# Row maxima of attention scores as pairs of 64-row matmuls on the two row halves of TensorE's array

## What is computed

```python
q = q.reshape(B * NUM_HEADS, S, hd)          # 8 heads of 64 values, S = 1024 tokens
k = k.reshape(B * NUM_HEADS, S, hd)
v = v.reshape(B * NUM_HEADS, S, hd)
scores = jnp.einsum('gqd,gkd->gqk', q, k) / jnp.sqrt(jnp.asarray(hd, x.dtype))
attn = jax.nn.softmax(scores, axis=-1)
wv = jnp.einsum('gqk,gkd->gqd', attn, v)
```

## Time and profile before

| | |
|---|---|
| median of 3 runs | 2581.28 us (2579.69 to 2582.69) |
| profiled execution, its time | 2579.7 us |
| profiled execution, its span | 2577.9 us |
| mean granted TensorE clock | 0.997 of full speed |
| busy share of PE, DVE, ACT, POOL | 97%, 75%, 44%, 44% |
| the chain that ended last: PE, DVE, issue, DMA | 86%, 5%, 2%, 2% |

### The profile page before, as it was taken

How to read it: one execution, slowest core, us unless ns; L and a number is a source line. 1 busy time by engine, 2 the same in 40 slices (tenths; PEclk the granted TensorE clock), 3 DMA queues, 4 the chain that set the end, 5 groups by cost and what they waited for, 6 DMA issues and landing times.

```text
span 2577.9 us, 39692 instructions
## 1 busy us (share of the span) xinstructions
PE 2501.4 (97%) x11720; PEld 987.6 (38%) x11720; DVE 1939.5 (75%) x2647; ACT 1141.6 (44%) x2059; POOL 1128.4 (44%) x971
## 2 busy tenths in 40 slices
PE   6999999999999999999999999999999999999999
PEld 2333333333333333333333333333344444444444
DVE  5887787778788787777878798976866966967515
ACT  4455555555545545555555554556232132132100
POOL 1366566556546746655664664655112021030000
PEclk9999999999999999999999999999999999999999
DMA  5234153242433315333342533332434634633534
GB/s 159 72 84 119 62 130 85 68 123 62 116 97 100 98 47 139 86 92 104 78 119 64 133 96 84 104 89 86 174 144 145 248 131 169 239 131 131 196 108 170
DMA packets 209915, 301.71 MB, mean 117 GB/s; under 512 B 82208, under 2 KB 131488, under 8 KB 209696
## 3 DMA queue, kind: packets, MB, share of 16 engines
q1 hardware_dynamic: 209424, 297.97, 38.9%
q10 hardware_dynamic: 272, 1.05, 0.1%
HBM read 195.54 MB, written 52.69 MB: 96 GB/s over the span
## 4 chain that ended last, share of the span: by engine, by line
PE 86%; DVE 5%; issue 2%; DMA 2%; ACT 1%; SPq 1%; POOL 1%; DVEq 0%; ACTq 0%; POOLq 0%
PE bank L846 29%; PE bank L752 16%; PE bank L726 14%; PE bank L687 11%; PE bank L705 8%; PE bank L697 6%; DVE nmax L1280 2%; PE bank L715 1%; DMA q_b<-shift 1%; DVE prob_sum L1274 1%; ACT prob L929 1%; PE bank L739 1%; SPq L419 1%; DVE qk_lo L1266 1%; DMA den_col<-den_sb 0%
## 5 line engine op out<-in xcount | busy, mean ns | idle before, releaser
L1280 DVE TENSOR_REDUCE nmax<-bank 128x1 f32<-128x512 f32 x1024 | 657.9, 682 | 231.7 <-PE bank L705 227.4
L929 ACT ACTIVATE prob<-bank 128x512 f32<-128x512 f32 x1024 | 560.7, 593 | 496.9 <-PE bank L726 492.5
L846 PE MATMUL bank<-v,u_slab 128*128 128x512 f16 x3456 | 746.9, 379 | 0.0
L1109 POOL TENSOR_TENSOR prob_sum<-prob_sum,prob 128x512 f32<-128x512 f32 x354 | 502.7, 1420 | 370.2 <-ACT prob L929 369.2
L752 PE MATMUL bank<-prob,val 128*64 128x512 f32 x2048 | 496.6, 606 | 0.0
L846 PEld LDWEIGHTS bank<-v,u_slab 128*128 128x128 f16 x3456 | 338.1, 98 | 407.0 <-issue 0.8
L705 PE MATMUL bank<-k_a,q_a 128*128 128x512 f16 x1024 | 384.2, 383 | 14.5 <-DVE nmax L1280 6.8
L1274 DVE TENSOR_TENSOR prob_sum<-prob_sum,prob 128x512 f32<-128x512 f32 x354 | 357.7, 1011 | 3.5 <-issue 0.3
L726 PE MATMUL bank<-q_a,k_a 128*128 128x512 f16 x1024 | 315.5, 381 | 16.6 <-ACT prob L929 15.0
L726 PE MATMUL bank<-q_b,k_b 128*128 128x512 f16 x1024 | 305.6, 380 | 9.0 <-DMA q_b<-shift 8.9
L752 PEld LDWEIGHTS bank<-prob,val 128*64 128x64 f32 x2048 | 124.3, 136 | 248.5 <-issue 206.4
(11 more groups left out here) (142 smaller groups left out, 2588.1 us busy)
## 6 DMA issues: line engine op xcount, KB each, us to landing
u_slab<-u_scratch SPq DMA_DIRECT2D x72, 1024.0 KB, 5.0
xs<-x SPq DMA_DIRECT2D x28, 1024.0 KB, 5.6
tile<-x_scratch SPq DMA_DIRECT2D x26, 1024.0 KB, 6.9
u_scratch<-u_w SPq DMA_DIRECT2D x96, 192.0 KB, 2.8
q_a<-qk_hi SPq DMA_DIRECT2D x64, 256.0 KB, 4.8
den_sb<-recip_scratch SPq DMA_DIRECT2D x128, 128.0 KB, 2.9
x_scratch<-xr SPq DMA_DIRECT2D x16, 1024.0 KB, 4.6
xr<-x SPq DMA_DIRECT2D x15, 1024.0 KB, 7.6
```

Source lines behind the costliest of these rows:

```text
L846: mm = pe.matmul(bank_at(pos, co)[:].rearrange("p (i n) -> p i n", i=2), slab[:, l, c, co * P:(co + 1) * P], image[v][:, 2 * c:2 * c + 2, ...
L929: act.activation(prob[:, (2 * u + e) % 8], sc_bank[bank_turn(s * 16 + 2 * u + e, 16 * HPI)[0]][:], ACT.Exp, scale=float(D) ** -0.5).then_i ...
L1109: nc.gpsimd.tensor_tensor(acc, in0, prob[:, (2 * kc + 1) % 8], ALU.add).then_inc(s1["sum1"], 1)
L1280: dve.tensor_reduce(nmax[:, m // 2, m % 2:m % 2 + 1], src[:], AX.X, ALU.max, negate=True)\
```

## The change

Each maximum tile now uses q's high part and k's high part only, 64 rows of products for a tile, and two tiles are issued one after the other: one on rows 0 to 63 (`k_b` against `q_a`), one on rows 64 to 127 (`k_a` against `q_a`), into two banks of the ring. For this the two parts of k change places in `k_a`; both halves of `q_a` hold the same, so the scores stay as they are. Places a and b are gone; `MAX_AT` puts a pair either at c (behind the unit's scores, ahead of d and of the burst) or at the new place e, behind the burst. DVE reduces two tiles for each pair.

```diff
-MAX_QUOTA = [2, 3, 3, 3, 3, 2, 0, 0]
+MAX_AT = {(0, "c"): 0, (0, "e"): 1, (1, "c"): 2, (2, "c"): 3, (2, "e"): 4, (3, "c"): 5, (4, "c"): 6, (4, "e"): 7}
...
-                hi_to = ((k_a, 0), (k_b, 0)) if which == 0 else ((q_a, 0), (q_a, D))
-                lo_to = (k_a, D) if which == 0 else (q_b, 0)
+                hi_to = ((k_a, D), (k_b, 0)) if which == 0 else ((q_a, 0), (q_a, D))
+                lo_to = (k_a, 0) if which == 0 else (q_b, 0)
...
-            def max_tile(s, m):
+            def max_pair(s, n):
 
                 half, tok = tokens(s)
-                dst = take()
-                pe.matmul(dst[:].rearrange("p (k t) -> p k t", t=TOK), q_a[half][:, m // 2, tok],
-                          k_a[half][:, 4 * (m % 2):4 * (m % 2) + 4, tok],
-                          start=True, stop=True).then_inc(s1["ring_full"], 1)
+                dst = take(), take()
+                for e, k_op in enumerate((k_b, k_a)):
+                    rows = slice(e * D, (e + 1) * D)
+                    pe.matmul(dst[e][:].rearrange("p (k t) -> p k t", t=TOK), q_a[half][rows, n, tok],
+                              k_op[half][rows, 4 * e:4 * e + 4, tok],
+                              start=True, stop=True).then_inc(s1["ring_full"], 1)
...
-                    run("a")
                     scores(h, s, u, 0)
-                    run("b")
                     if u == 0:
                         pe.wait_ge(s1["shift_row"], 16 * (h + 1))
                     scores(h, s, u, 1)
...
+                    run("e")
...
-                    for place in "abcd":
+                    if u == 1 and den_direct(s - 1, more):
+                        den_from_bank(h - 1)
+                    for place in "cde":
...
-                                max_item(h + 1, a)
+                                max_item(h + 1, 2 * a)
+                                max_item(h + 1, 2 * a + 1)
```

More of the change, by code:

```diff
@@ L102, in ring_items @@
 def ring_items(u, nxt, prev, v_units, stat):
-    first = sum(MAX_QUOTA[:u])
-    tiles = [("max", first + k) for k in range(MAX_QUOTA[u])] if nxt else []
-    at = {"a": tiles[0:1], "b": tiles[1:2], "c": tiles[2:]}
+    at = {place: [("max", MAX_AT[u, place])] if nxt and (u, place) in MAX_AT else [] for place in "ce"}
     at["d"] = [("value", u // 2)] if v_units and u % 2 else []
@@ L774, in run @@
                             if kind == "max":
-                                max_tile((s + 1) % HPI, a)
+                                max_pair((s + 1) % HPI, a)
                             elif kind == "value":
@@ L814, in _ @@
             pe.wait_ge(s1["qk_moved"], 192)
-            for m in range(16):
-                max_tile(0, m)
-                if m % 4 == 1:
-                    project_qk(1, 1, 0, m // 4)
+            for n in range(SEG):
+                max_pair(0, n)
+                if n % 2 == 0:
+                    project_qk(1, 1, 0, n // 2)
             slot(0, 0, prev=False)
@@ L1569, in slot @@
                             add_tile(h, s, u - 1)
-                        if place == "a" and u == 1 and den_direct(s - 1, more):
-                            den_from_bank(h - 1)
                         if place == "d" and u in (1, 2) and (s == 0 and ahead or s == 1 and more):
```

## The result

The changed kernel takes 2681.04 us (median of 4 runs, 2673.84 to 2685.36) where the kernel before takes 2581.04 beside it: ratio 1.0384, 95% interval 1.0360 to 1.0408. It is slower by 100 us; the prediction said 2600, in a range of 2554 to 2635. The sign was right, the size was a fifth of what came.

What follows compares the result with a forecast made beforehand. The prediction took PE as setting the pace, with DVE close in some slots. Slot terms summed to +2.5 us an image; six images +15 and the last two +5, on 2579.7, gave 2600, range 2554 to 2635.

Steps and rivals of the forecast that it cites:

- The price of a pair: On PE: two row-half matmuls run together in 0.23 us, and each change of the array's division costs 0.10.
- the gain of the quiet slots: Slots 4, 5, 2 and 6: the late reciprocal is covered, so they gain 0.6, 0.6, 0.5 and 0.5 us.
- The halves overlap: On PE: assumed in the sum; the rival without overlap said slower, 2665 us at most, chance 0.10.
- the one of free changes: Rival on PE: row halves change for less than 0.10 us, faster, 2560 or 2518, chance 0.12.
- Pair 5's wait for the ring: Slots 0 and 1: DVE reaches pair 4 late, so pair 5 waits for a bank, +0.75 us each.
- what the new order makes late: Main term: DVE's later reciprocal delays SP's queue and the shift; PE waits 3.5, 0.7, 1.3, 0.8 us in slots 1, 0, 3, 7.
- The lateness is harmless: Rival: the shift still lands in time in slots 0, 1, 3 and 7; faster, 2558 us, chance 0.20.
- the price of the lateness: Net change forecast per slot: +2.4 us in slot 1, +0.8 in 0, +1.0 in 3, +0.5 in 7.
- level with it: Slot 1, DVE: the reciprocal, 2.8 us ahead of the last burst before, would end together with that burst.
- the denominators' item: Slots 3 and 7, on PE: this item waits 0.16 us for a ring bank, part of why PE gains only 0.3.
- in any case: Slot 0: PE loses 0.80 us at the branch of the loop over images, whatever the change does.
- +5 for two: Last two images, where DVE also has the convolution's first tiles: 0 to +8 us, taken as 5.

Runs made afterwards that it cites:

- e3: The kernel before with only its reciprocal moved late, behind unit 5's last maxima: 2661.22 us, ratio 1.0335.
- e1: The changed kernel with the reciprocal moved early again, ahead of the reductions of unit 4's last pair: 2602.55 us, ratio 1.0082.
- e12: The changed kernel with only slot 0's 1 MB load issued behind the shift's send: 2663.43 us, ratio 1.0322.
- e5: The changed kernel with extra, later overwritten score products issued ahead of slots 2, 0 and 4 to fill the shift waits: 2674.36 us, ratio 1.0366.
- e10: e4 with the last image's maxima as full products in the places of the kernel before, and its reciprocal at the end of unit 4: 2583.18 us, ratio 1.0014.
- e6: The changed kernel, reciprocal still late, with the 1 MB loads of slots 0 and 1 issued behind the shift's send: 2625.76 us, ratio 1.0182.
- e4: e1 with the 1 MB loads of slots 0 and 1 issued behind the shift's send: 2596.05 us, ratio 1.0065.
- e11: e10 with pairs only in slots 2, 4, 5 and 6, the other slots having the maxima of the kernel before: 2563.82 us, ratio 0.9939.
- e9: The kernel before with only the 1 MB loads of slots 0 and 1 issued behind the shift's send: 2579.44 us, ratio 0.9994.

## Why the prediction came out wrong

**Right.** The price of a pair (0.22) and of a change (0.10); the gain of the quiet slots, -0.6 forecast and -0.7 measured in 4 and 5, -0.4 in 6. The halves overlap, so that rival is gone, and the one of free changes too. Pair 5's wait for the ring in slots 0 and 1, 0.75 forecast: it is 0.69 idle in both slots in every image from the second to the sixth. The row in slot 0 has 0.69, or 0.76 start to start (1008.43 - 1007.14 - 0.53):

```profile
1007.14 0.59 PE L726 MATMUL bank<-q_b,k_b 128*128 128x512 f16 x2
1008.43 0.39 PE L705 MATMUL bank<-k_b,q_a 64*128 64x512 f16 x1 [0.69 <-DVE nmax L1279]
```

The main term, "what the new order makes late", named the right mechanism, and in slots 1, 3 and 7 the right wait: e3 shows that lateness alone makes +82, e1 that taking it away returns the loop to 218.8. In slot 0 another wait counts: the reciprocal ends 1.8 ahead of the last burst (1.3 was written), and in the five passages with a gap at the branch PE does not wait for the shift at all, where 0.7 was forecast; it waits 1.3 only at the sixth, which has no gap. So slot 0's +2.8 is in the main the longer gap (2.6 to 3.0 idle for 0.8 to 1.6) and pair 5's wait. "The lateness is harmless" (0.20) was wrong.

**The step that failed: the price of the lateness**, forecast at 2.4, 0.8, 1.0 and 0.5 in slots 1, 0, 3 and 7, measured as 5.9, 2.8, 2.9 and 2.5. Six things were missing from it or sized too small.

- *The reciprocal came later than walked.* Against the last burst it ends 0.6 after in slot 1 (1053.98 - 1053.40; "level with it" was written) and 0.4 after in slots 3 and 7 (0.1 was written). So the shift waits, by the starts, are 4.3 to 4.7 in slot 1 (3.5), 1.5 to 2.2 in slot 3 (1.3) and 1.8 to 2.2 in slot 7 (0.8). Part of it is in the walk through DVE's queue: a split of 1.58 stands ahead of the reciprocal in slot 1, where the kernel before has 0.68 in the same place. (The prediction's own terms for slot 1, a landing at 10.0 and a need at 6.3, make 3.7 and not 3.5.)
- *The shift lands later.* The prediction gave it 2.2 in slots 3 and 7. It takes 2.1 to 2.8 from slot 3 and 2.9 to 3.2 from slot 7 in the loop. In slot 7 this is the larger part of the miss: 0.7 to 1.0, where the late reciprocal has 0.3.
- *The ring in slot 3.* The prediction had 0.16 for the denominators' item. That wait is there (0.19), but pairs 1 and 2 wait too: 0.7 to 1.1 in all.
- *The loop's branch.* The prediction had 0.80 there "in any case". It is not a constant: it changes with how long ahead the load was issued, and a late reciprocal moves the load to the worst of the four places seen. e12, which moves that load alone, takes 18 us off.
- *The clock.* Behind each of slot 1's shift waits (4.2 us and more) and each of the five gaps at the branch TensorE's granted clock is 0.5, which is 1.2 GHz, for a while. Behind the shorter waits (1.0 to 2.1 idle) it is so in three of seven images in slot 7 and in two of seven in slot 3. It costs 1.7 us in slot 2 alone (e5), and up to 5.2 in the image shown (PE's busy time). Over the whole execution the granted clock is 0.981 against 0.997, so the low clock has 43 of the 100 us at most. That is how slot 2, forecast at -0.5, came to +1.3. The Trainium skill ("TensorE: Matmul & The Clock Gate", "HAM oscillation — how this bites in real kernels") describes such a case, a wait for a DMA that lets the clock fall, so that the stage behind it starts at half rate every time; the trace agrees behind slot 1, with a burst of 3.68 for 1.94. It belonged in the sum as soon as a wait of 3.5 was forecast.
- *The last images.* +5 for two was taken by feel; it was +25 (19.6 and 5.3). e10 shows that 11 (by the table) to 13 (by the runs) of it are the places of the maxima in the last image. The 5.3 of the last but one are the lateness, since e1 has only 0.5 there.

What the 100 us are, by the runs in this order (in the other order, e1 ahead of e4, the reciprocal has 78 and the loads 6.5): 55 are the loads behind which a late reciprocal puts the shift and the branch's fetch (e6); 30 more the late reciprocal by itself (e6 to e4, 2625.8 to 2596.1); 13 the last image (e4 to e10); and 3 remain, since the last image is still 4.9 longer, while in the loop the pairs' gain in slots 2, 4, 5 and 6 is spent again in slots 1, 3 and 7 (218.7 against 218.8). In slot 3, even with the reciprocal early, pairs cost 1.4 (21.1 against 19.7; e11 has 19.8 with full tiles). e4's trace has 1.0 there in waits for ring banks and 0.5 in a wait for the shift, neither of which the kernel before has; the waits for the exponentials, which the prediction named, are the same as before (0.4 to 0.5 idle in all).

## What to carry to other kernels

Before moving work on an engine, list what it pushes back in that engine's queue, then what stands behind *that* in the DMA queue: here an instruction of 0.19 us, two steps off the moved work, decided 78 of 100 us. A small transfer that an engine waits for goes ahead of a large load: worth 55 us here where it was late, 6.5 (e4) and nothing (e9) where it was early. A forecast wait of several microseconds on TensorE had a second price here, the lower clock behind it. And a change that gains in some stages and loses in others is best applied to those stages alone, read from a table of periods by stage (e11).

## What the runs showed of the hardware

- Two 64-row float16 matmuls of 512 columns on the two row halves start 3 ns apart and together take the time of one full-array matmul. Changing the division costs 0.09 to 0.10 us each way between the full array and row halves, and 0.09 into column halves; out of the burst it is up to 0.14, on to row halves as on to the full array.
- The gap at the loop's branch went from 0.1 to 0.5 us (e6) to 2.8 to 3.1 in two programs that differ only in when the 1 MB loads are issued (slot 0's 2.3 us ahead of the last matmul, or 4.1). Where the same branch is not taken, it is 0.
- Behind waits of 2.7 us at the branch and 4.5 us for the shift the granted clock fell to its lower level: 0.92 and 0.94 over slots 1 and 2, where e11 has 1.00 in all of the slots shown. Behind the shift waits of 1.0 to 2.1 in slots 3 and 7 it did so in five cases of fourteen.
- The shift's 2 KB transfer, issued 0.13 us behind two broadcasts of 128 KB each in the same queue, took 2.98 us to land; issued 1.66 us behind a load of 1 MB, 5.24.
